# Two reorderings in a fused attention and mixture-of-experts kernel: where a weight half is split, and when a token group is transposed

## The reference

```python
router_logits = x @ w_gate                            # 8 experts
topk_w, topk_ids = lax.top_k(softmax(router_logits), 2)
combine = ...                                         # the two weights, normalised, per expert
gu = einsum('th,ehf->etf', x, w_gate_up)              # per expert 512 -> 2 * 256
eo = einsum('eti,eih->eth', silu(g) * u, w_down)      # 256 -> 512
routed = einsum('te,eth->th', combine, eo)
shared = silu_and_mul(x @ w_sh_gate_up) @ w_sh_down   # 512 -> 2 * 1024, 1024 -> 512
out = layernorm(x + routed + shared)
```

## Time and profile before

| | |
|---|---|
| median of three runs | 709.66 us (709.5 to 709.79) |
| the profiled execution: time, span | 709.05 us, 707.2 us |
| TensorE (PE) matmul busy | 687.8 us, 97% |
| VectorE (DVE) | 431.0 us, 61% |
| ScalarE (ACT) | 316.8 us, 45% |
| GpSimd (POOL) | 303.7 us, 43% |
| mean granted TensorE clock | 0.996 |
| DMA | 92.08 MB, mean 130 GB/s |

### The profile page before, as it was taken

How to read it: one execution, slowest core, us unless ns; L and a number is a source line. 1 busy time by engine, 2 the same in 40 slices (tenths; PEclk the granted TensorE clock), 3 DMA queues, 4 the chain that set the end, 5 groups by cost and what they waited for, 6 DMA issues and landing times.

```text
span 707.2 us, 16608 instructions
## 1 busy us (share of the span) xinstructions
PE 687.8 (97%) x7004; PEld 561.1 (79%) x7004; DVE 431.0 (61%) x721; ACT 316.8 (45%) x606; POOL 303.7 (43%) x342
## 2 busy tenths in 40 slices
PE   9999999999999999999999999999999999999994
PEld 7777888878877777887888788888887888888883
DVE  4897565486664545378884646444565447767555
ACT  5653444455545543252111557556666552141232
POOL 2657555667645533101002444435444136526232
PEclk9999999999999999999999999999999999999998
DMA  8221131123342414000053576678447766414212
GB/s 278 81 78 44 64 121 62 56 70 121 107 127 86 136 47 150 30 29 1 0 191 110 164 237 227 251 256 306 137 165 268 240 221 208 117 62 120 75 75 89
DMA packets 54190, 92.08 MB, mean 130 GB/s; under 512 B 5152, under 2 KB 20256, under 8 KB 54112
## 3 DMA queue, kind: packets, MB, share of 16 engines
q1 hardware_dynamic: 48432, 72.36, 29.5%
q0 software_dynamic: 5680, 18.62, 9.1%
HBM read 67.36 MB, written 23.59 MB: 129 GB/s over the span
## 4 chain that ended last, share of the span: by engine, by line
PE 80%; DVE 10%; ACT 3%; issue 2%; POOL 1%; DMA 1%; SPq 1%; POOLq 0%; DVEq 0%; ACTq 0%
PE bank L763 20%; PE bank L1282 12%; PE bank L787 9%; PE bank L450 9%; PE bank L1334 7%; PE bank L655 7%; PE bank L579 4%; PE bank L554 4%; PE bank L1256 2%; PE bank L1303 2%; PE bank L692 2%; DVE x L790 1%; PE bank L624 1%; DMA RAW<-in_wvT 1%; DVE sg L739 1%
## 5 line engine op out<-in xcount | busy, mean ns | idle before, releaser
L236 POOL TENSOR_TENSOR xl<-RAW,xh 128x1024 fp32r<-128x1024 f32 x23 | 55.5, 2412 | 115.9 <-ACT xh L235 85.9
L763 PE MATMUL bank<-XH,GH 128*128 128x512 f32 x256 | 101.8, 398 | 0.6 <-DVE GL L248 0.3
L259 ACT ACTIVATE ah<-sg 128x512 fp32r<-128x512 f32 x48 | 30.3, 632 | 156.3 <-DVE sg L739 154.1
L763 PE MATMUL bank<-XH,GL 128*128 128x512 f32 x256 | 99.9, 390 | 0.0
L763 PE MATMUL bank<-XL,GH 128*128 128x512 f32 x256 | 99.7, 389 | 0.0
L739 DVE TENSOR_TENSOR sg<-sg,bank 128x512 f32<-128x512 f32 x48 | 32.9, 685 | 80.5 <-PE bank L1282 42.5
L1148 POOL DMA_INDIRECT xg<-x1d,idxu x39 | 42.1, 1079 | 72.3 <-DVE idxu L1124 41.3
L597 POOL TENSOR_SCALAR rstd<-mv 128x1 f32<-128x1 f32 x48 | 15.3, 319 | 134.4 <-DVE mv L596 133.6
L565 DVE TENSOR_TENSOR r<-bank,vst 128x256 f32<-128x256 f32 x64 | 26.5, 422 | 68.0 <-PE bank L554 67.3
L260 DVE TENSOR_TENSOR GL<-RAW,GH 128x1024 fp32r<-128x1024 f32 (+2 forms) x47 | 53.2, 1156 | 11.6 <-ACT GH L259 10.2
L568 ACT ACTIVATE r<-r,mask 128x128 f32<-128x128 f32 x128 | 41.0, 391 | 42.3 <-DVE r L565 42.3
(11 more groups left out here) (227 smaller groups left out, 1653.1 us busy)
## 6 DMA issues: line engine op xcount, KB each, us to landing
RAW<-in_wgu SPq DMA_DIRECT2D x13, 1024.0 KB
yd<-RAW SPq DMA_DIRECT2D x39, 256.0 KB
RAW<-in_wsgu SPq DMA_DIRECT2D x14, 512.0 KB
RAW<-in_wd SPq DMA_DIRECT2D x13, 512.0 KB
x<-in_xtok SPq DMA_DIRECT2D x16, 256.0 KB, 3.2
x1d<-x SPq DMA_DIRECT2D x16, 256.0 KB, 2.3
RAW<-in_wsd SPq DMA_DIRECT2D x8, 512.0 KB
out_x<-x SPq DMA_DIRECT2D x16, 256.0 KB, 2.0
```

What stands on the lines that cost most here:

```text
L236: b = PO.op(lambda e: e.tensor_tensor(DL[:, p, :, :], draw[:, rawp(w), :, :], DH[:, p, :, :].bitcast(F32), ALU.subtract), a, dloaded[w], *f)
L763: t = PE.op(lambda e, b=b, k=k, c=c, wt=wt, xx=xx, n=n: e.matmul(bank[b][:], wt[:, p, k, c:c + 128], xx[h][:, k, :], start=(n == 1), stop= ...
```

## The change

Slot 64 transposes only blocks 4 and 5, into banks 0 and 1, and slot 65 blocks 6 and 7, into banks 2 and 3, behind that slot's `hi_z(15)`, `norm_two(14)` and `t_one(15)`, and ahead of the down steps that fill it. Before the routed jobs, the first half of the first job's weights is split behind strip 1 instead of strip 0, and the second half behind all four strips and the last down step instead of behind strip 1; `load_gate(6)` is issued after the loop.

```diff
@@ slot(n) @@
                 for h in (0, 1):
                     free[h], free[2 + h] = (rtok[h],), (gdone[31, h],)
-                for i in range(4, 8):
-                    turn_x(i, base=i // 2 % 2 * 2)
+                for i in (4, 5):
+                    turn_x(i, base=0)
                 load(3)
+            if n == 65:
+                for i in (6, 7):
+                    turn_x(i, base=2)
             if n == LAST:
@@ before the routed jobs @@
             if n == 0:
                 first_turns = turn_r(0, (0, 1, 2, 3))
             next(first_turns, None)
-            if n < 2:
-                split_g(4, (2 * n,))
-            if n == 1:
-                load_gate(6)
             if n == 2:
                 next(first_turns)
+            if n % 2:
+                split_g(4, (n - 1,))
+        load_gate(6)
         split_d(4)
```

## The result

The changed kernel took 712.04 us (median of 8 executions, 710.48 to 712.45) against 709.41 for the kernel before (8 executions, 708.75 to 709.79): a ratio of 1.0034, interval 1.0023 to 1.0044, so it is 2.4 us slower (1.6 to 3.1). The forecast was 710.6, within 708.5 to 711.1. It missed by 1.4.

A forecast was written before the change was run, and what follows sets the result against it. TensorE, busy almost the whole span, was taken as the bound, so only its waits matter. Slot 64's -0.78 and the routed weights' +1.72 sum to +0.94 us, on the median of 709.66 giving 710.6, range 708.5 to 711.1.

The forecast's parts named there:

- Slot 64: Moving blocks 6 and 7 removes TensorE's 0.99 us wait, adds one for `XL7`: second token group starts 0.78 us earlier.
- the second place: TensorE's wait before the first routed product, 1.7 us in the kernel before; slot 64's 0.78 us gain should arrive there.
- The order of `xl` and `GL`: Before the routed jobs, GpSimd's `xl` starts about 0.3 us ahead of VectorE's second-half `GL`, which then reads about 3.2.
- The seventh product: First routed product needing the second weight half; it waits for `GL` and starts at 399.25 instead of 397.56, 1.69 us later.
- the restart: TensorE resuming after its wait at the seventh routed product: a few hundredths of a us more, making the loss 1.72.
- VectorE comes first: Rival before the routed jobs: `xl` starts over 0.3 us later or `GL` earlier, `GL` runs free; 708.6 us, chance 0.19.
- Slower: Rival: overlap as forecast, but slot 64's gain is lost as `XH6` and `XH7` wait behind `norm_two`; 711.4 us, chance 0.05.

The follow-up runs named there:

- the ordered kernel: The whole change, with GpSimd's `xl` of the first routed down weights made to wait for the second half's `GL`: 708.3 us, ratio 0.9986.
- the filled wait: The whole change, plus eight 512-column products with an unused result while TensorE waits at the seventh routed product: 710.74 us, ratio 1.0023.
- the halved `xl`: The whole change, with GpSimd's first routed `xl` done as two operations of half the size: 709.29 us, ratio 1.0002.

## Why the prediction missed

*Slot 64.* Right, in mechanism and in size: a gain of 0.78 was forecast, 0.74 came. The wait moved from the down product to the last `XL`, behind `norm_two`. It arrived at the second place, within the scatter of some 0.3 that the stretch between has, and slot 64 alone has it in its total. That the place of blocks 6 and 7 behind the stages of slot 65 is what holds it back is shown by the run with them ahead (1.19, where 1.15 was expected); that it is `norm_two` among these is read from ScalarE's rows.

*The order of `xl` and `GL`.* Right. `xl` was forecast to start about 0.3 ahead and started 0.21 ahead, the stretched gather of 1.56 included; `GL` was to read about 3.2 and read 3.25; its end was to come 1.07 after `xl`'s and came 1.08 after. The seventh product was forecast 1.69 later and is 1.75 later. That the order alone decides is shown from both sides, by the added wait and by the first half left in place.

*The step that failed: the restart.* The sum ended at the seventh product: "the stage costs 399.25 - 397.56 = 1.69, a few hundredths more for the restart: **loss 1.72**". For what follows the wait it had a few hundredths. In the profiled execution the 18 products behind the wait took 5.81 instead of 4.11, +1.70, about as much as the 1.75 that the wait had cost: 0.10 is the restart at full speed, as the second profile of the same kernel shows, and 1.60 comes from the eight products that ran at half the clock. The trace before has no row of products behind such a wait: its longest wait of TensorE is 1.69, the clock stands at 1.00 through it, and I took that for the behaviour after one of 2.1 as well. It did have a fall in view, the one at the end of the span shown above, within 4 us of the last product, and I didn't ask what such a fall would cost further up. Half speed should have stood in the range as its upper end: with the 1.6 now measured that is 711.1 + 1.6 = 712.7, which holds the result.

*How sure the clock is as the cause.* Two things show it: the filled wait, with the clock at 1.00 and none of its 11 executions with a second fall, though work was added; and the two profiles of one program, with 5.81 and 4.21 for the same 18 products. The total of a kernel with the long wait is a mixture: by the stages' starts the change costs -0.74 + 1.75 + 0.10 = 1.1 without the fall and 2.7 with it, and the measured 2.4 lies between. What decides whether it falls is open. The end of the span shows that chance has a part: there the fall came between 2.1 and 5.3 us after TensorE's last product, in profiles whose ends are the same work.

*The rivals.* "VectorE comes first" was close to true, 0.21 us away: had `xl` started that much later, for example behind a gather stretched further, `GL` would have run free as in the ordered kernel, at 708.3. The prediction held against it that a lead of 0.14 had been enough "in both" cases of its rows; it was 0.14 in one and 0.78 in the other. "Slower" had the right side, for a reason that played no part.

## What to carry to other kernels

Before moving an operation, look at what will run beside it on the other of VectorE and GpSimd: if both read two operands from SBUF, the one that started second was held here until the first was over, and 0.2 us of order was worth 2.0 us at TensorE's seventh product (12.44 against 10.40). Put the operation that TensorE waits for first, by its place or by an explicit wait of the other. And where a forecast gives TensorE a longer wait than any in the trace around it, count the wait and, as the upper end, half-speed products behind it: here 1.6 us, in some executions and not in others. A fall of 3 us doesn't show in slices of 18; the spacing of the products' starts shows it.

## What the runs showed of the hardware that was not expected

- The granted clock fell to 0.51 for about 3.4 us behind waits of 2.14 (the changed kernel) and 2.17 us (the weights part alone), and did not behind waits of 2.16 and 2.17 us in two further profiles, nor behind 1.69 before or 1.08 with the halved `xl`. In one of the falls two products ran at full speed first.
- At the end of the span, with no product left, the clock fell 2.1 to 5.3 us after the last one, differently in each of the twelve profiles.
- A `GL` holds up an indirect DMA on GpSimd too. The issue of a gather takes 0.95; in each of the twelve profiles all seven gathers between 388 and 535 us that began 0.2 to 0.9 us into a `GL` ended 0.80 to 0.83 after the `GL` did, whatever their start, and so took 1.12 to 1.85. Those that began within 0.02 of the `GL`'s start took 0.95. In the kernel before (VectorE, then GpSimd):

```profile
438.31 1.23 DVE L260 TENSOR_TENSOR GL<-RAW,GH 128x1024 fp32r<-128x1024 f32 x1 [1.33 <-ACT GH L259]
```

```profile
438.76 1.59 POOL L1148 DMA_INDIRECT xg<-x1d,idxu  x1 [0.31 <-issue]
```

It hardly moved the start of `xl` in the changed kernel, 395.29: the gathers ended at 395.26, but the copy `xh` that `xl` needs ended at 395.19, so an unstretched gather would have let it start less than 0.1 earlier.
